# Attention scores from stacked float16 halves in place of float32 products

## The reference

```python
q = split_heads(x @ Wq + bq)       # 16 heads of 16 features
k = split_heads(x @ Wk + bk)
v = split_heads(x @ Wv + bv)
# 7 windows of 128 tokens, 64 apart; the last is counted twice
scores = einsum('bhnqd,bhnkd->bhnqk', qw, kw) / sqrt(16) + pos_bias
ow = einsum('bhnqk,bhnkd->bhnqd', softmax(scores), vw)
# overlapping windows are added up and divided by their counts, then @ Wo + bo
```

## Time and profile before

| | us |
|---|---|
| three timed runs | 1558.44, 1553.88, 1556.32 |
| median | 1556.32 |
| span of the profiled execution, first to last instruction | 1558.5 |
| of it PE busy | 1341.3 |
| DVE busy | 924.5 |
| ACT busy | 645.8 |
| POOL busy | 246.7 |

### The profile page before, as it was taken

The page is one execution under the profiler, slowest core; times in us unless marked ns, Lnnn a source line. Parts: engine busy times, 40 slices in busy tenths (PEclk is TensorE's granted clock), DMA queues, the critical chain, the costliest instruction groups (busy, mean ns, idle before and its releaser), DMA issues.

```text
span 1558.5 us, 32504 instructions
## 1 busy us (share of the span) xinstructions
PE 1341.3 (86%) x8323; PEld 858.5 (55%) x8324; DVE 924.5 (59%) x3760; ACT 645.8 (41%) x2323; POOL 246.7 (16%) x279
## 2 busy tenths in 40 slices
PE   4412799999996899989899999989994699999996
PEld 4411466666664456656566565656653366666664
DVE  5789444444443567787687877787784244444442
ACT  1114322232222476656566665656661132222221
POOL 4323001000102101021111112020212101100100
PEclk9999999999998899999999999999996799999998
DMA  9500442000002101020201111020206221000000
GB/s 301 206 28 31 171 151 58 13 13 13 17 13 88 48 21 42 22 56 21 57 9 38 33 32 46 21 56 21 56 9 242 59 58 55 17 13 13 13 17 14
DMA packets 57278, 85.55 MB, mean 55 GB/s; under 512 B 8848, under 2 KB 40848, under 8 KB 57168
## 3 DMA queue, kind: packets, MB, share of 16 engines
q1 hardware_dynamic: 50352, 65.49, 13.7%
q0 software_dynamic: 6816, 18.81, 3.4%
HBM read 45.81 MB, written 27.97 MB: 47 GB/s over the span
## 4 chain that ended last, share of the span: by engine, by line
PE 66%; DVE 12%; issue 6%; ACT 2%; POOL 2%; DMA 1%; SPq 1%; another core or an unknown queue 1%; DVEq 0%; ACTq 0%; POOLq 0%
PE bank L797 24%; PE bank L926 9%; PE bank L749 9%; PE bank L815 9%; PE bank L952 6%; PE bank L886 4%; DVE w_all L1364 3%; DVE w_all L1373 2%; PE bank L912 2%; DVE hb L1210 2%; PE bank L963 2%; ACT sl L629 2%; PE bank L763 1%; PE bank L899 1%; POOL sorted_rows L504 1%
## 5 line engine op out<-in xcount | busy, mean ns | idle before, releaser
L709 ACT ACTIVATE w_all<-w_all 128x128 f32<-128x128 f32 x896 | 349.7, 393 | 223.1 <-DVE w_all L1364 222.0
L797 PE MATMUL bank<-w_all,xt 128*128 x1680 | 391.2, 383 | 11.5 <-DVE xt L1222 3.5
L1364 DVE CUSTOM_DVE_ANT_0 w_all<-bank,w_all 128x128 f32<-128x128 f32 x896 | 207.3, 287 | 133.8 <-PE bank L926 123.5
L797 PEld LDWEIGHTS bank<-w_all,xt 128*128 128x128 f16 x1680 | 165.3, 98 | 196.7 <-issue 37.3
L1210 DVE SCALAR_TENSOR_TENSOR hb<-bank,ew,sl 128x512 f32<-128x512 f32 x140 | 105.1, 751 | 207.2 <-ACT sl L629 207.2
L815 PE MATMUL bank<-w_all,ht 128*128 x1680 | 206.2, 273 | 1.2 <-DVE yt L1235 1.2
L629 ACT ACTIVATE sl<-bank,back 128x512 f32<-128x512 f32 x140 | 95.9, 685 | 238.6 <-PE bank L797 221.8
L749 PEld LDWEIGHTS bank<-ident,w_all 128*128 128x128 f32 x896 | 112.6, 142 | 119.9 <-issue 113.2
L815 PEld LDWEIGHTS bank<-w_all,ht 128*128 128x128 f16 x1680 | 164.2, 98 | 19.4 <-issue 1.7
L709 ACT ACTIVATION_READ_ACCUMULATOR w_all<-w_all 128x1 f32 x896 | 169.8, 189 | 0.0
L1373 DVE COPY w_all<-bank 128x512 f32<-128x512 f32 x224 | 153.7, 686 | 1.3 <-PE bank L749 1.2
(11 more groups left out here) (163 smaller groups left out, 1585.5 us busy)
## 6 DMA issues: line engine op xcount, KB each, us to landing
big<-sorted_rows SPq DMA_DIRECT2D x70, 130.5 KB
saved<-w_all SPq DMA_DIRECT2D x16, 512.0 KB
w_all<-saved SPq DMA_DIRECT2D x4, 2048.0 KB, 14.2
w_all<-mid SPq DMA_DIRECT2D x9, 512.0 KB, 3.6
big<-in_L_attn_hidden_states SPq DMA_DIRECT2D x8, 512.0 KB, 4.2
w_all<-in_L_ffn_gate_w SPq DMA_DIRECT2D x8, 512.0 KB
w_all<-in_L_ffn_up_w SPq DMA_DIRECT2D x8, 512.0 KB
w_all<-in_L_ffn_down_w SPq DMA_DIRECT2D x8, 512.0 KB
```

Source lines behind the costliest of these rows:

```text
L709: a = nc.scalar.activation(prob[:, u % NB, h], sbias[:, u % NB, h], ACT.Exp, bias=nmax[:, u % NB, h:h + 1], scale=-1.0, accum_out=rsum[:, ...
L797: mm = nc.tensor.matmul(bank[2 * e + w][:], xt[:, hx, c, :], flat(gu16[:, bass.ds(g * E + e, 1), w, hw, c, :]), start=(i == 0), stop=(i == ...
L1364: i = nc.vector.tensor_tensor_reduce(out=sbias[:, u % NB, h], in0=bank[u % 2][:, h * W:(h + 1) * W], in1=nbias[:, (u % NQ) * HQ + h], scal ...
```

## The change

- Queries and keys are split in a high and a low float16 part. ACT writes the high part (`high_k`, `high_q`), DVE then the low one, the projection minus the high part (`low_k`, `low_q`).
- SP spreads them over 96 partitions for a pair of heads: keys as high, low, high (`spread_keys`, 24 copies), queries as high, high, low (`spread_queries`, 12 copies), into tiles for each parity of the batch. One float16 product over 96 rows then sums high x high, high x low and low x high. A unit has two such products, each with 256 columns, where it had one float32 product with 512.
- A unit's four heads are taken from other places, so that a pair stands where the copies need it (`head`); the products with the values of a unit now go to four groups of 32 output partitions, and two units add to the same place, where they went to two groups with two heads each.
- The first scores of a batch wait for all 36 copies.
- The value projections all use bank 6 (`V_BANK`), so that each waits for the copy of the one before it.
- The biases and weights of queries and keys are scaled by powers of two, found from their largest elements: Wq, Wk and, in 32 small loads, bq and bk are loaded at the start of the kernel, their largest elements go into the step that finds the scales of the experts' weights (`scales`), and DVE scales them in 16 small operations after the experts.
- Half of `SIDE` is moved.

```diff
@@ SIDE
-                12: ("k0", "copy_k0"),
-                13: ("k1", "r_norm0", "copy_k1"),
-                14: ("r_norm1",),
-                16: ("turn_route",),
-                17: ("copy_route",),
-                19: ("logits", "q0", "copy_q0"),
-                20: ("q1", "copy_q1"),
-                21: ("choose0",),
-                22: ("choose1", "v0"),
-                23: ("rank", "copy_v0"),
-                24: ("choose2", "v1"),
-                25: ("choose3", "place", "copy_v1"),
-                26: ("v2",),
-                27: ("v3", "copy_v2", "copy_v3")}
+                12: ("k0", "high_k0"),
+                13: ("k1", "high_k1", "r_norm0"),
+                14: ("low_k0", "r_norm1"),
+                15: ("q0", "high_q0", "low_k1"),
+                16: ("q1", "high_q1"),
+                17: ("low_q0",),
+                18: ("low_q1",),
+                19: ("turn_route", "copy_route"),
+                21: ("logits",),
+                22: ("v0",),
+                23: ("v1", "choose0", "copy_v0"),
+                24: ("v2", "choose1", "copy_v1"),
+                25: ("v3", "rank", "copy_v2"),
+                26: ("choose2", "copy_v3"),
+                27: ("choose3", "place")}
@@ SP
-            def mask_keys(b, half):
-                cols = slice(half * S // 2, (half + 1) * S // 2)
-                km2 = km.rearrange("p (c h) s -> p c h s", c=DC)
-                for h in range(HC):
-                    r = HD * h
-                    sp.dma_start(km2[r:r + HD, :, h, cols], kt[r:r + HD, :, cols]).then_inc(km_loaded[half], 16)
+            def spread_keys(par):
+                for q in range(NQ):
+                    for t, part_ in enumerate((0, 1, 0)):
+                        for h in range(2):
+                            r, r2 = 2 * HD * q + HD * h, 2 * HD * t + HD * h
+                            sp.dma_start(km[par][r2:r2 + HD, q * HQ + h:(q + 1) * HQ:2, :],
+                                         kt[r:r + HD, part_]).then_inc(km_loaded, 16)
+            def spread_queries(par):
+                for q in range(NQ):
+                    for t, part_ in enumerate((0, 0, 1)):
+                        r, r2 = 2 * HD * q, 2 * HD * t
+                        sp.dma_start(qs[par][r2:r2 + 2 * HD, q * DC:(q + 1) * DC, :],
+                                     qt[r:r + 2 * HD, part_]).then_inc(qs_loaded, 16)
...
                     sp.wait_ge(k_ready, b * DC + 2 * DC)
-                    sp.wait_ge(s_done, b * UNITS + 4 * NQ + OPEN)
-                    mask_keys(b + 1, 0)
+                    sp.wait_ge(s_done, b * UNITS + OPEN)
+                    spread_keys(1 - par)
+                    sp.wait_ge(q_ready, b * DC + 2 * DC)
+                    spread_queries(1 - par)
                     sp.wait_ge(xa_ready, (prep_use(b + 1) + 1) * TB)
                     load_batch(b + 2)
                     shift_values(b + 1, 1 - par)
-                    sp.wait_ge(s_done, b * UNITS + UNITS + OPEN)
-                    mask_keys(b + 1, 1)
@@ PE
-                if t in (0, 2):
-                    pe.wait_ge(q_ready, b * DC + (t // 2 + 1))
+                if t == 0:
+                    pe.wait_ge(q_ready, b * DC + 1)
...
-                    pe.wait_ge(v_ready, b * TB + (1 if t == 1 else 2))
+                    pe.wait_ge(v_ready, b * TB + t)
...
-                nc.tensor.matmul(bank[u % 2][:].rearrange("p (h k) -> p h k", h=HQ),
-                                 qt[par][:, q * HQ // HC, n * STRIDE:n * STRIDE + W],
-                                 km[:, q * HQ:(q + 1) * HQ, n * STRIDE:n * STRIDE + W],
-                                 start=True, stop=True).then_inc(s_done, 1)
+                for m in range(DC):
+                    mm = nc.tensor.matmul(bank[u % 2][:, 2 * m * W:2 * (m + 1) * W].rearrange("p (h k) -> p h k", h=2),
+                                          qs[par][0:KR, q * DC + m, n * STRIDE:n * STRIDE + W],
+                                          km[par][0:KR, q * HQ + 2 * m:q * HQ + 2 * m + 2, n * STRIDE:n * STRIDE + W],
+                                          start=True, stop=True)
+                mm.then_inc(s_done, 1)
...
-                    m, pair = divmod((q * HQ + h) // 2, HC // 2)
-                    mm = nc.tensor.matmul(bank[4 + (par + n) % 2][HS * pair:HS * (pair + 1), m * W:(m + 1) * W],
-                                          va[par][:, n, q * HQ + h, :], pt_s[:, u % 2, h * W:(h + 1) * W],
-                                          start=(h % 2 == 0), stop=(h % 2 == 1))
+                    m, odd = divmod(q, 2)
+                    mm = nc.tensor.matmul(bank[4 + (par + n) % 2][HS * h:HS * (h + 1), m * W:(m + 1) * W],
+                                          va[par][:, n, head(u, h), :], pt_s[:, u % 2, h * W:(h + 1) * W],
+                                          start=(odd == 0), stop=(odd == 1))
@@ DVE
+            def low_k(b, m):
+                dve.wait_ge(k_high, b * DC + (m + 1))
+                nc.vector.scalar_tensor_tensor(out=kt[:, 1, m, :], in0=bank[6 + m][:], scalar=qkb[:, 1, m:m + 1], in1=kt[:, 0, m, :],
+                                               op0=ALU.add, op1=ALU.subtract).then_inc(k_ready, 1)
@@ POOL
-                    if n == (3 if last else 4) and not first_:
+                    if n == (3 if last else 5) and not first_:
                         scatter(b + (B - 1), route_use(b - 1), stage, B, scattered[1])
```

More of the change, by code:

```diff
@@ L32 @@
 NQ = H // HQ
+NPAIR = H // 2
+TERMS = 3
+KR = TERMS * 2 * HD
 UNITS = NWIN * NQ
@@ L50 @@
 EXPONENT = 0x7F800000
-SCALE_STEPS = 7
+SCALE_STEPS = 8
 LOOK = (4, 5)
@@ L153, in macaron_kernel @@
         wmax = sb("wmax", [P, NMAT])
-        wm = sb("wm", [P, 3])
-        wmt = sb("wmt", [3, 4])
-        w_pow = sb("w_pow", [P, 3])
-        w_inv = sb("w_inv", [P, 3])
+        qk_max = sb("qk_max", [P, 4])
+        wm = sb("wm", [P, NSPAN])
+        wmt = sb("wmt", [NSPAN, NSPAN + 1])
+        w_pow = sb("w_pow", [P, NSPAN])
+        w_inv = sb("w_inv", [P, NSPAN])
+        qk_ratio = sb("qk_ratio", [P, 2])
+        qk_scale = sb("qk_scale", [P, 2])
+        qk_first = stage[:].rearrange("p t r -> p (t r)")
         w_scale = sb("w_scale", [P, 3])
@@ L293, in macaron_kernel @@
                      22: ("choose3", "place")}
-        PREP = ("stats0", "stats1", "norm0", "norm1", "turn_prep", "copy_prep", "k0", "k1", "copy_k0",
-                "copy_k1", "q0", "q1", "copy_q0", "copy_q1", "v0", "v1", "v2", "v3",
+        PREP = ("stats0", "stats1", "norm0", "norm1", "turn_prep", "copy_prep", "k0", "k1", "high_k0",
+                "high_k1", "low_k0", "low_k1", "q0", "q1", "high_q0", "high_q1", "low_q0", "low_q1", "v0", "v1", "v2", "v3",
                 "copy_v0", "copy_v1", "copy_v2", "copy_v3")
@@ L331, in _ @@
         def _(sp):
-            for s in km_loaded:
-                sp.sem_inc(s, OPEN)
             def load_x(r, par):
@@ L866, in _ @@
             pe.wait_ge(wmax_found, 1)
-            nc.tensor.transpose(bank[4][0:3, 0:P], wm[:], ident[:]).then_inc(wmax_turned, 1)
+            nc.tensor.transpose(bank[4][0:NSPAN, 0:P], wm[:], ident[:]).then_inc(wmax_turned, 1)
             pe.wait_ge(wmax_diag, 1)
-            nc.tensor.matmul(bank[5][:, 0:3], ones[0:3, :], wmt[:, 1:4], start=True, stop=True).then_inc(wmax_spread, 1)
+            nc.tensor.matmul(bank[5][:, 0:NSPAN], ones[0:NSPAN, :], wmt[:, 1:NSPAN + 1], start=True, stop=True).then_inc(wmax_spread, 1)
             with pe.Fori(SPLIT[0], B - 1) as r:
@@ L1016, in batch @@
                         if s == "rank":
-                            if not last:
-                                pe.wait_ge(q_ready, b * DC + (DC + 2))
                             rank(b + (B - 1), bank[7])
@@ L1337, in _ @@
             dve.wait_ge(y_ready, NS + OPEN)
-            nc.vector.memset(km[:, 0:H // 2], 0.0).then_inc(km_zero, 1)
+            nc.vector.memset(big[:, 0:H * S // 2], 0.0).then_inc(km_zero, 1)
+            dve.wait_ge(root_ready, 1)
+            step = Chain(qk_step, 0)
+            step(nc.vector.tensor_single_scalar(qk_scale[:, 0:1].bitcast(I32), qk_ratio[:, 1:2].bitcast(I32), EXPONENT, ALU.bitwise_and))
+            nc.vector.reciprocal(qk_scale[:, 1:2], qk_scale[:, 0:1])
+            step(nc.vector.tensor_scalar(qk_ratio[:, 0:1], qk_scale[:, 0:1], -1.0 / HD ** 0.5, None, ALU.mult))
+            nc.vector.tensor_scalar(qkb[:, 2, :], qkb[:, 0, :], qk_ratio[:, 0:1], None, ALU.mult)
+            nc.vector.tensor_scalar(qkb[:, 1, :], qkb[:, 1, :], qk_scale[:, 1:2], None, ALU.mult)
+            dve.wait_ge(w_saved, 16 * NGU)
+            for k, dst, by in ((1, wk_s, qk_scale[:, 1:2]), (0, wq_s, qk_ratio[:, 0:1])):
+                for c in range(DC):
+                    for m in range(DC):
+                        at_ = (k * DC + c) * D
+                        for a in range(2):
+                            i = nc.vector.tensor_scalar(in_pairs(dst[:, c, :], m, a), by_pairs(qk_first[:, at_:at_ + D], m, a), by, None,
```

(12 more changed lines are left out.)

147 lines of the change are left out of this document (87 added, 60 removed).

## The result

The changed kernel takes 1549.7 us (median of 20 runs, 1545.0 to 1558.5), the kernel before 1554.1 in the 20 runs beside them (1549.2 to 1558.4): a ratio of 0.9971, 95% interval 0.9959 to 0.9982. Forecast were 1522 and -34.8 us. The sign was right, but only an eighth of the gain came. The profiled executions are 12.0 us apart (spans 1558.5 and 1546.5), more than the medians.

The account below looks back on a forecast made before the run. PE bounded the batches, with DVE next and the limit after the change. Batches -56.7, before the first scores +20.3, ahead of the expert layer +1.6: -34.8 us, so 1522 us; 8-in-10 range 1494 to 1564.

Parts of the forecast that it names:

- The copies ahead of the first scores: Before the first scores: all 36 copies must land, 0.68 us each to issue, 18.3 us more on the path.
- the 2.0 for the clock: Before the first scores: PE idles 18 us and then starts at its lower clock level, counted as 2.0 us.
- the copies are hidden in the middle batches: End of middle batches: copies take 26.5 us against 29 of DVE time, so hidden by 2 to 3 us.
- the copy rival: SP's queue of copies is the bound, at 0.97 us a copy: slower, 1590 us; chance 12%.
- The places where PE is late on top: Units 6, 21 and 22: PE side steps exceed what DVE's work hides, by 0.8, 1.0 and 1.2, together 3.0 us.
- DVE's work of a batch: Middle batch: DVE, with 2.8 us of low parts added, is busy 65.3 us, 66.1 as span, the batch's floor.
- Placing and the loop's turn: End of a middle batch: later placing costs 0.7 us, stalls at the loop's turn stay at 1.2.
- Batch 0: First batch: 67.9 us for 76.4, 8.5 less, with about 3 us of its copies showing.
- Values in one bank: Value projections 1 to 3 each wait for DVE's copy, DVE idling 1.4 us each time; 4.7 a batch, ends 0 and 5.5.
- The clock rival: PE at the low clock for a third of the batches' time: about +10 us a batch, 1600 us; chance 5%.
- Gains eaten: Engines hand over worse than counted in units with steps on both, 4 us a batch: 1554 us; chance 11%.
- The faster rival: PE keeps further ahead: value projections' waits half overlap, the three late places vanish; batch 70.4 us, kernel 1480; chance 15%.

Follow-up runs that it names:

- the run with the high parts first alone: Changed kernel with, in the loop, the 16 key copies of high parts issued before the 8 of low parts; 1550.0 us, ratio 0.9980.
- the run with the waits filled: Changed kernel with six unused float32 products on PE ahead of each wait for the copies of value projections 0 and 1; 1541.2 us, ratio 0.9925.
- The spread run: Changed kernel with value projections spread over units 22, 23, 24 and 26, the second in bank 7, their copies in other units; 1526.7 us, ratio 0.9828.

## Why the prediction was wrong

**Right, with sizes.** The copies ahead of the first scores: 36 at 0.65 (0.68 taken). With the scales 19.9 us were forecast up to the first scores, and 19.1 came (545.7 - 526.6); the 2.0 for the clock belong behind them and went into batch 0. That the copies are hidden in the middle batches, and that the copy rival (1590) is not what happens: shown by the run with the high parts first alone. The places where PE is late on top: DVE idles 0.80 us in unit 6 and 0.99 in unit 21, forecast 0.8 and 1.0. DVE's work of a batch, 65.2 for 65.3. Placing and the loop's turn: 2.0 us idle in units 26 and 27, forecast 1.9. Batch 0: 64.5 for 67.9, better by 3.4.

**Failed: "Values in one bank", and the clock beside it.** It gave the three projections 4.7 us a batch. DVE idles 7.9 in units 23 to 25, and 1.9 in unit 22 where 1.2 stood. The two make 3.9 of the 4.7 us by which a middle batch misses its forecast in this count (80.4 for 75.7). 3.9 times six is 23 of the 27 us by which the stretch from the first scores to the first output product misses (652.5 - 623.0 = 29.5 less in the profiles, 56.7 forecast). The rest is waits of 0.2 to 0.5 in some units of the middle batches, the last batch, 4.4 longer than forecast (63.0 to its first scatter for 58.6, which ends 0.9 ahead of it), and the tail's 1.1, less the 3.4 of batch 0.

The greater part of it is a step that the forecast didn't price: it took PE's durations at the full clock and left the clock to a rival with 5%, on the strength of the stretch 690 to 700. That stretch was of a kernel in which PE hardly waited; the same stretch after has 0.74. By the table above, the low clock makes 2.0 of the 7.9, which the run with the waits filled confirms (DVE's idle time in units 23 to 25 went to 6.1), and 0.9 of the 1.9 in unit 22: together 2.9 us a batch, 17 of the 27. No run took the 0.9 away; it is read from the two batches in which projection 0 ran at the full clock.

The smaller part is the hand-over within the term: at the full clock units 23 to 25 still idle 5.9, 1.2 over the forecast. In the row shown one turn of the chain takes 1.64 us in place of the 1.4 taken (the 1.22 and 0.25 behind that figure are 1.47 when added up).

The spread run shows the term's full weight: of DVE's 9.8 us of idle time in units 22 to 25 it took 5.7. The prediction had seen this wait, and had it bounded by 5.5 a batch; measured it is 7.9, outside the bounds, since the bounds came from rows at the full clock, at which it is 5.9.

**The clock rival** named 1600, with +10 us a batch, if a third of the batches' time ran at the low level. That condition nearly came true, 28%, and PE's busy time is 64.2 where 61 was forecast; but the price was 2.9 us a batch and not 10, since more than half of that time lies where DVE hardly waits for PE (units 0 to 4 idle 0.4 us together). *TensorE: Matmul & The Clock Gate* of the Trainium skill, section "HAM oscillation", says that idle gaps throw the engine back to the low clock. The trace agrees for projection 2: behind waits of 2.9 to 3.7 us it is slow in all six batches (1.9 to 2.1 us for 1.13). For projection 1, behind waits hardly shorter, it agrees in three batches of six, and ahead of the low clock from 828 to 832 stand only waits of under 0.5 us. Part 3 of the same page, on packing small matmuls, would have halved the values' 0.57; eight of them take 0.40 in the chain of the changed kernel, so the rule holds in part.

**Gains eaten** (1554, 11%) comes nearest in its time, but not in its mechanism: it has the engines hand over worse in all units, and the excess sits in four. The faster rival (1480, 15%) had the waits of the value projections half gone; they came longer than forecast.

Open: why the granted clock is low at projection 0 or 1 in one batch and not in the next, why it stays low for 10 us and more around the turn of the batches, and what makes one kernel's runs differ by 13 us (1545 to 1558).

## What to carry to other kernels

When a change turns an engine that never waited into one that waits, price its work behind each wait at both clock levels, and bound the range with both. Price it place by place: here 22 us of a batch ran at the low level and 2.9 of loss came of it, and the mean clock was the same in two kernels that lie 23 us apart. A buffer that is written, copied out and written again costs its hand-over on two engines each time it comes round within one step; a second buffer, and a copy made a step before the next writing needs it, take most of it out (here 23 us). And when one wait goes, look at once for the transfer that was hidden behind it: here 19 to 23 us more lay in the start of 16 small copies, which alone were worth nothing.

## What the runs showed of the hardware

Products that nobody needs, six in each of two waits of PE a batch, made the kernel 7 to 8.5 us faster and raised the mean clock of the batches from 0.86 to 0.91, while every score product doubled made it 23 slower and left the clock at 0.87, though PE had more busy time there (404.13 us of 480) than with the wait filled (392.31). The clock can be low while the engine is busy: in 828 to 832 it is 0.58 with PE busy 4.00 of 4 us, and in 819 to 823, with PE busy 2.92 of 4, it is 1.00. A small copy between tiles costs its queue 0.63 to 0.71 us of issue, on ScalarE's queue (3.54 for 5, 7.08 for 11) as on SyncE's (12.46 for 19, 7.55 for 12), and the two queues run side by side.
